# adaLN block with two products: hardware loops written out, the half block's down projection as row pairs

## What is computed

```python
h = layernorm(x) * (1 + ca) + sa
attn = einsum('ds,td->st', w1, w2) * sparse_mask
x = x + ga * gelu(h @ attn + b2)
h = layernorm(x) * (1 + cb) + sb
H = (h @ U1) @ V1 + b1            # U1 1024x256, V1 256x5504
act = silu(H[..., :2752]) * H[..., 2752:]
out = (act @ U2) @ V2 + b2        # U2 2752x256, V2 256x1024
x = x + gb * out
```

## Time and profile before

| what | us |
|---|---|
| median of 3 runs | 1254.88 (1254.66 to 1256.98) |
| the profiled execution | 1254.12 |
| its span, first to last instruction | 1252.3 |
| mean granted TensorE clock over the span | 0.989 of full speed |
| PE busy | 1193.5 (95%), 5617 matmuls |
| DVE busy | 672.5 (54%) |
| ACT busy | 402.4 (32%) |
| POOL busy | 320.1 (26%) |

### The profile page before, as it was taken

One profiled execution on the slowest core, in us unless ns is written; L12 is line 12 of the kernel. 1 busy time (PEld: TensorE's weight loads), 2 busy tenths in 40 slices (PEclk: granted clock), 3 DMA queues, 4 the chain that ended last, 5 costly groups with the idle time before them and its releaser, 6 DMA issues.

```text
span 1252.3 us, 15955 instructions
## 1 busy us (share of the span) xinstructions
PE 1193.5 (95%) x5617; PEld 952.4 (76%) x5617; DVE 672.5 (54%) x1041; ACT 402.4 (32%) x675; POOL 320.1 (26%) x256
## 2 busy tenths in 40 slices
PE   7877999999999899999999999999999999999997
PEld 4445678877786678788888878878877888887885
DVE  0838699999996544543543443353353354345344
ACT  0122334344343364413322313322331332232331
POOL 0023221332323175600420240060060042024014
PEclk9999899999999899999999999999999999999999
DMA  9796635535448464250141042024015013104101
GB/s 344 289 379 243 260 142 195 231 140 223 168 176 301 155 187 170 68 168 1 51 137 49 17 140 80 1 91 144 1 68 169 1 51 135 51 16 140 47 1 68
DMA packets 54064, 165.79 MB, mean 132 GB/s; under 512 B 4976, under 2 KB 9456, under 8 KB 51952
## 3 DMA queue, kind: packets, MB, share of 16 engines
q1 hardware_dynamic: 54000, 164.86, 36.3%
HBM read 122.84 MB, written 42.01 MB: 132 GB/s over the span
## 4 chain that ended last, share of the span: by engine, by line
PE 84%; DVE 8%; DMA 3%; issue 2%; ACT 1%; SPq 1%; POOL 1%; DVEq 0%; ACTq 0%
PE bank L492 26%; PE bank L494 25%; PE bank L493 25%; PE bank L562 4%; DVE nrm L1054 2%; PE bank L658 2%; DMA x<-in_x 2%; PE bank L527 1%; DVE bn L1212 1%; DMA wm_sb<-in_wmod 1%; DVE h_lo L1155 1%; DVE bn L1044 1%; POOL g L1330 1%; DVE xr L1207 1%; ACT h_hi L875 0%
## 5 line engine op out<-in xcount | busy, mean ns | idle before, releaser
L1269 DVE SCALAR_TENSOR_TENSOR act<-bank,b_sb,act 128x512 f32<-128x512 f32 (+1 forms) x176 | 132.0, 750 | 393.3 <-PE bank L494 378.0
L982 ACT ACTIVATE act<-bank,b_sb 128x512 f32<-128x512 f32 (+1 forms) x176 | 121.2, 689 | 516.8 <-PE bank L494 511.8
L492 PE MATMUL bank<-pt,v_hi 128*128 128x512 f32 x688 | 269.4, 392 | 5.9 <-issue 4.4
L493 PE MATMUL bank<-pt,v_hi 128*128 128x512 f32 x688 | 268.4, 390 | 0.0
L494 PE MATMUL bank<-pt,v_lo 128*128 128x512 f32 x688 | 268.4, 390 | 0.0
L1383 POOL TENSOR_TENSOR v_lo<-v2g,v_hi 128x512 fp32r<-128x512 f32 x32 | 41.4, 1294 | 567.8 <-ACT v_hi L998 567.8
L1276 DVE TENSOR_TENSOR act_lo<-act,act_hi 128x512 fp32r<-128x512 f32 (+1 forms) x176 | 172.7, 985 | 0.0
L492 PEld LDWEIGHTS bank<-pt,v_hi 128*128 128x128 f32 x688 | 129.4, 188 | 36.4 <-issue 7.7
L494 PEld LDWEIGHTS bank<-pt,v_lo 128*128 128x128 f32 x688 | 129.5, 188 | 26.9
L493 PEld LDWEIGHTS bank<-pt,v_hi 128*128 128x128 f32 x688 | 129.4, 188 | 26.8
L492 PE MATMUL bank<-act_hi,u_hi 128*128 128x512 f32 (+1 forms) x352 | 139.3, 396 | 1.5 <-DVE act_lo L1276 1.3
(11 more groups left out here) (114 smaller groups left out, 1571.6 us busy)
## 6 DMA issues: line engine op xcount, KB each, us to landing
wm_sb<-in_wmod SPq DMA_DIRECT2D x10, 2048.0 KB, 12.3
xr<-in_x SPq DMA_DIRECT2D x16, 1024.0 KB, 6.8
x_dram<-xr SPq DMA_DIRECT2D x16, 1024.0 KB, 4.3
x2t<-x_dram SPq DMA_DIRECT2D x32, 512.0 KB, 4.0
out<-x2t SPq DMA_DIRECT2D x32, 512.0 KB, 4.7
xs<-in_x SPq DMA_DIRECT2D x7, 2048.0 KB, 8.0
pt_dram<-pt_st SPq DMA_DIRECT2D x8, 1024.0 KB, 3.9
pt<-pt_dram SPq DMA_DIRECT2D x8, 1024.0 KB, 6.8
```

What stands on the lines that cost most here:

```text
L492: nc.tensor.matmul(acc, s_hi, m_hi, start=start, stop=False)
L493: nc.tensor.matmul(acc, s_hi, m_lo, start=False, stop=False)
L982: nc.scalar.activation(act[0:w, i % 2, :], bank[0:w, i % 2, :], ACT.Silu, bias=b1_sb[0:w, i, 0:1]).then_inc(silu_done, 1)
L1269: nc.vector.scalar_tensor_tensor(act[0:w, i % 2, :], up, b1_sb[0:w, i, 1:2], act[0:w, i % 2, :], ALU.add, ALU.mult).then_inc(act_done, 1)
```

## The change

Every `Fori` on every engine becomes a Python `range`: the same instructions are issued, each batch's one behind the other, with constants in place of registers in waits and addresses, and no branch back. In the FFN phase the half block's z product is issued in another form. Today both r use rows 0 to 63 of U2's last block and of act. After the change the second 128 columns of that U2 block lie in rows 64 to 127, and act_hi and act_lo hold the 64 rows twice, in partitions 0 to 63 and 64 to 127. The six matmuls are issued by term, in three pairs: r = 0 on rows 0 to 63 into bank 4, r = 1 on rows 64 to 127 into bank 5. For the copies ACT issues one more act_hi copy and DVE one more act_lo subtraction in each batch, each before the one that raises the semaphore. The last U2 piece is loaded in two parts (64 rows x 128 columns each) instead of one, with one copy (ACT) and one subtraction (POOL) for each.

```diff
--- before.py
+++ after.py
@@ -241,6 +241,7 @@
         raw_in = [sem(f"raw_in{i}") for i in range(3)]
         w_hi_ready = sem("w_hi_ready")
         w_ready = sem("w_ready")
+        half_lo_ready = sem("half_lo_ready")
         pt_in = [sem("pt_in0"), sem("pt_in1")]
         gate_done = sem("gate_done")
         up_done = sem("up_done")
@@ -321,16 +322,21 @@
             parts = [(u2[a:a + full * P, :].rearrange("(i p) r -> p i r", p=P), P, full, R, 0,
                       u2_hi[:, i0:i0 + full, :], u2_lo[:, i0:i0 + full, :])]
             if rest:
-                parts.append((u2[a + full * P:e, :].rearrange("(i p) r -> p i r", i=1), rest, 1, R, full * R,
-                              u2_hi[0:rest, i0 + full:i0 + full + 1, :],
-                              u2_lo[0:rest, i0 + full:i0 + full + 1, :]))
+                for r in range(RB):
+                    cols, rows = slice(r * P, (r + 1) * P), slice(r * rest, (r + 1) * rest)
+                    parts.append((u2[a + full * P:e, cols].rearrange("(i p) r -> p i r", i=1), rows, 1, P, full * R,
+                                  u2_hi[rows, i0 + full:i0 + full + 1, cols],
+                                  u2_lo[rows, i0 + full:i0 + full + 1, cols]))
             pieces.append(parts)
             piece_of["u2", q] = len(pieces)
         PIECES = len(pieces)
+        HALF_PIECE = piece_of["u2", len(GROUPS) - 1] - 1
 
         def raw_part(slot, part):
             _, rows, blocks, n, off, _, _ = part
-            return raw[0:rows, slot, off:off + blocks * n].rearrange("p (k n) -> p k n", k=blocks)
+            if isinstance(rows, int):
+                rows = slice(0, rows)
+            return raw[rows, slot, off:off + blocks * n].rearrange("p (k n) -> p k n", k=blocks)
 
         raw_count = []
         seen = [0, 0, 0]
@@ -418,7 +424,7 @@
                     sp.dma_start(x2_store[b, :, TT // 2:TT, :], xr[:, TT // 2:TT, :]).then_inc(x2_out, 16)
 
             iteration(0, True, False, True, (6, 7, 8, 9))
-            with sp.Fori(1, NB - 2) as b:
+            for b in range(1, NB - 2):
                 iteration(b, True, True, True)
             iteration(NB - 2, True, True, False, (10,))
             iteration(NB - 1, True, True, False, (), True)
@@ -478,7 +484,7 @@
             for n in range(TT):
                 tile_in(0, n)
             batch(0, 0, False)
-            with sp.Fori(1, NB // 2) as i:
+            for i in range(1, NB // 2):
                 batch(i * 2 - 1, 1, False)
                 batch(i * 2, 0, False)
             batch(NB - 1, 1, True)
@@ -737,7 +743,7 @@
 
             iteration(0, True, False, True)
             iteration(1, True, True, True)
-            with pe.Fori(2, NB - 1) as b:
+            for b in range(2, NB - 1):
                 iteration(b, True, True, True)
             iteration(NB - 1, True, True, False)
 
@@ -785,10 +791,18 @@
                     pe.wait_ge(z_lo_ready, b * 2)
                 w = width[i]
                 slot = (q * IB + i) % 4
-                for r in range(RB):
-                    cols = slice(r * P, (r + 1) * P)
-                    last = three(bank[:, 4 + r, :], u2_hi[0:w, i, cols], u2_lo[0:w, i, cols],
-                                 act_hi[0:w, slot, :], act_lo[0:w, slot, :], i == 0, i == IB - 1)
+                if w == P:
+                    for r in range(RB):
+                        cols = slice(r * P, (r + 1) * P)
+                        last = three(bank[:, 4 + r, :], u2_hi[:, i, cols], u2_lo[:, i, cols],
+                                     act_hi[:, slot, :], act_lo[:, slot, :], i == 0, False)
+                else:
+                    terms = ((u2_hi, act_hi), (u2_hi, act_lo), (u2_lo, act_hi))
+                    for t, (weight, moving) in enumerate(terms):
+                        for r in range(RB):
+                            rows = slice(r * w, (r + 1) * w)
+                            last = nc.tensor.matmul(bank[:, 4 + r, :], weight[rows, i, r * P:(r + 1) * P],
+                                                    moving[rows, slot, :], start=False, stop=t == len(terms) - 1)
                 last.then_inc(z_step, 1)
 
             def out_product(b):
@@ -840,7 +854,7 @@
                 pe.wait_ge(lo_ready, turn2(NB - 1) + FB)
                 up_product(0, 0, i)
             batch(0, 0, False)
-            with pe.Fori(1, NB // 2) as i:
+            for i in range(1, NB // 2):
                 batch(i * 2 - 1, 1, False)
                 batch(i * 2, 0, False)
             batch(NB - 1, 1, True)
@@ -968,7 +982,7 @@
             shift_hi(0)
             iteration(0, True, False, True)
             iteration(1, True, True, True)
-            with ae.Fori(2, NB - 1) as b:
+            for b in range(2, NB - 1):
                 iteration(b, True, True, True)
             iteration(NB - 1, True, True, False)
             iteration(NB, False, True, False)
@@ -988,6 +1002,8 @@
                 ae.wait_ge(act_done, b * IB + i + 1)
                 if not at_start(b, i < 4):
                     ae.wait_ge(z_step, b * IB + max(i - 3, 0))
+                if w < P:
+                    nc.scalar.activation(act_hi[w:P, slot, :], act[0:w, i % 2, :], ACT.Copy)
                 nc.scalar.activation(act_hi[0:w, slot, :], act[0:w, i % 2, :], ACT.Copy).then_inc(act_hi_ready, 1)
 
             def v2_hi_part(b, part):
@@ -1016,7 +1032,7 @@
 
             silu(0, 0, 0)
             batch(0, 0, False)
-            with ae.Fori(1, NB // 2) as i:
+            for i in range(1, NB // 2):
                 batch(i * 2 - 1, 1, False)
                 batch(i * 2, 0, False)
             batch(NB - 1, 1, True)
@@ -1245,7 +1261,7 @@
                                     b2_sb[:].unsqueeze(2).to_broadcast([P, FB, NB]), ALU.add).then_inc(table_ready, 1)
             iteration(0, True, False, True)
             iteration(1, True, True, True)
-            with dve.Fori(2, NB - 1) as b:
+            for b in range(2, NB - 1):
                 iteration(b, True, True, True)
             iteration(NB - 1, True, True, False)
             dve.wait_ge(gb_turned, 1)
@@ -1273,6 +1289,9 @@
                 w = width[i]
                 slot = (q * IB + i) % 4
                 dve.wait_ge(act_hi_ready, b * IB + i + 1)
+                if w < P:
+                    nc.vector.tensor_tensor(act_lo[w:P, slot, :], act[0:w, i % 2, :], act_hi[0:w, slot, :],
+                                            ALU.subtract)
                 nc.vector.tensor_tensor(act_lo[0:w, slot, :], act[0:w, i % 2, :], act_hi[0:w, slot, :],
                                         ALU.subtract).then_inc(act_lo_ready, 1)
 
@@ -1302,7 +1321,7 @@
             multiply(0, 0, 1)
             act_lo_part(0, 0, 0)
             batch(0, 0, False)
-            with dve.Fori(1, NB // 2) as i:
+            for i in range(1, NB // 2):
                 batch(i * 2 - 1, 1, False)
                 batch(i * 2, 0, False)
             batch(NB - 1, 1, True)
@@ -1347,8 +1366,15 @@
                 for n, part in enumerate(pieces[m]):
 
                     pool.wait_ge(w_hi_ready, sum(len(p) for p in pieces[:m]) + n + 1)
+                    if not isinstance(part[1], int) and part[1].start:
+                        pool.wait_ge(w_ready, m)
+                        pool.wait_ge(half_lo_ready, n)
                     last = nc.gpsimd.tensor_tensor(part[6], raw_part(m % 3, part), part[5], ALU.subtract)
+                    if m == HALF_PIECE and n < len(pieces[m]) - 1:
+                        last.then_inc(half_lo_ready, 1)
                 last.then_inc(w_ready, 1)
+                if m == HALF_PIECE:
+                    pool.wait_ge(w_ready, m + 1)
 
 
             def iteration(b, has_next):
@@ -1364,7 +1390,7 @@
                 rstd(mv2, ve2, rstd2, mv2_ready, b * 4 + 4, b * 2 + 3 if has_next else b * 2 + 2, rstd2_ready)
 
             iteration(0, True)
-            with pool.Fori(1, NB - 1) as b:
+            for b in range(1, NB - 1):
                 iteration(b, True)
             iteration(NB - 1, False)
 
@@ -1393,7 +1419,7 @@
                     nc.gpsimd.tensor_tensor(half, gbb2_bc[:, h * HALF:(h + 1) * HALF], half,
                                             ALU.add).then_inc(x2_biased, 1)
 
-            with pool.Fori(0, NB) as b:
+            for b in range(NB):
                 gate_v2(b)
                 bias_x2(b)
 
```

## The result

The changed kernel takes **1263.85 us** (median of 4 runs, 1262.04 to 1265.25); the kernel before took 1254.77 beside it (median of 4, 1254.20 to 1256.98). The ratio is 1.0068, 95% interval 1.0054 to 1.0082: slower by 7 to 10 us. The forecast was 1258.8, slower, with 1249 to 1266 as its range. The profiled execution is the slowest of the four: 1265.25 us, span 1263.5, against 1254.12 and 1252.3 before.

What follows compares the result with a forecast made beforehand. TensorE, 84% of the chain, was taken to bound the kernel. Subtractions +13.5, clock +2.3, row pairs -4.7 and loops -6.4 us sum to +4.7 on the profiled 1254.12 us: 1258.8 us, range 1249 to 1266.

Steps and rivals of the forecast that it cites:

- The third subtraction: VectorE's extra act_lo subtraction before the half block, entering TensorE's path in full: 1.69 us a batch, +13.5 us.
- the sum of 15.8 us: Alternative estimate from the skill's port-lock rule for the eight extra VectorE subtractions, 1.97 us each.
- The loops of the FFN phase: TensorE's two FFN loop turns: gaps regained, 4.9 us, and a clock drop avoided, 1.5 us; together -6.4 us.
- Rival (d): Written-out code doesn't help, TensorE waits for instructions elsewhere as often: +11.1 us, 1265.2 us; chance 0.05.
- The pairs: TensorE's half-block products on two 64-row halves at once: 0.59 us gained a batch, -4.7 us in eight.
- The estimate of 0.48: Half-block gain per batch if a row pair gained 1.54x, from the skill's four-tile figure; 3.8 us in eight.
- rival (b): Row halves of the half block's product don't overlap on TensorE: the 4.7 us are missing, 1263.5 us; chance 0.15.
- The ScalarE copy at nothing: ScalarE's extra half-block copy ends while VectorE is busy with block 20: cost nothing; without cover 0.5 us a batch.
- The clock again: TensorE's longer waits before block 21 bring one or two clock drops in eight, 1.5 us each: +2.3, bounds 0 and 12.
- rival (a): The clock holds in every TensorE pause: +2.4 us, 1256.5 us; chance 0.20. Against it, small gaps around each change of shape.
- 4 turns give nothing: TensorE's attention-phase loop turns fall where it waits for normalised rows anyway: no gain; without cover at most 2.4 us.

Runs made afterwards that it cites:

- copies_only: loops_only plus ScalarE's and VectorE's second copy of the half block in every batch, read by nobody, product in its old form: 1281.97 us, ratio 1.0209.
- bias_late: The changed kernel with one more GpSimd wait, so a batch's adds to x2t start only after its last act_lo subtraction: 1244.98 us, ratio 0.9921.
- loops_only: The kernel before with every hardware loop written out as a Python range, nothing else changed: 1249.32 us, ratio 0.9944.
- pe_ffn_loop: The kernel before with only TensorE's FFN loop written out: 1247.84 us, ratio 0.9948.
- order_only: The changed kernel with ScalarE's two half-block copies in the other order, the upper rows' copy with its own semaphore: 1264.35 us, ratio 1.0067.
- bias_late_order: order_only plus the GpSimd wait of bias_late: 1242.13 us, ratio 0.9891.
- filler: The changed kernel with seven useless matmuls on TensorE before its wait for the half block's act_lo: 1258.04 us (median of 7), ratio 1.0028.
- best: bias_late_order with hardware loops back everywhere except TensorE's FFN loop: 1239.98 us, ratio 0.9871.
- pairs_no_copies: The changed kernel without the extra ScalarE copy and VectorE subtraction per batch, output not the wanted one: 1245.33 us, ratio 0.9916.

## Why the prediction was right, and where it was not

**The sign, and its reason, hold.** The time is 5 us above the forecast and inside its range. The third subtraction stands on TensorE's path: forecast 1.69 us a batch, measured 1.67 to 1.68 in the profile after, and copies_only shows the stall without the pairs. That GpSimd's adds make it dear is shown by bias_late, which changes nothing but their time. The rule of the Trainium skill ("SBUF — State Buffer", "SBUF: two separate sides") that the loser waits a whole instruction out would have had 1.97 us, by the estimate of the prediction; the trace has 1.67 between the ends of the two subtractions. That the two engines hold each other up at this place the runs confirm (both are slower together, and both recover in bias_late); the sum of 15.8 us they don't.

**The loops of the FFN phase: right.** -6.4 forecast, -6.5 in loops_only's FFN phase, -6.7 in pe_ffn_loop as a whole. Rival (d) has fallen.

**The pairs: a little undersized.** 0.59 us forecast, 0.71 measured, outside the upper end of 0.68 that I gave: the stream is at that end (three steps of 0.227 instead of six), and the change of shape costs 0.21 instead of 0.24. The two halves of a pair are not 0.11 us apart; they start together. The estimate of 0.48 from the four-tile figure in the section on the span model of "TensorE: Matmul & The Clock Gate" in the Trainium skill is further off: for two 64-row tiles the trace has the stream halved, a gain of 2x. The result lies at rival (b)'s 1263.5, but its mechanism is wrong: pairs do overlap.

**The ScalarE copy at nothing: right**, and for the reason named: VectorE's cover. order_only shows it, and bias_late_order shows its price once that cover is gone: 0.35 us a batch, where 0.5 was written.

**What failed is "The clock again".** It had one or two drops in eight stalls, +2.3 us. The profile has four stalls with drops and +6.2 us against before with the turn's drop counted off, that is 7.7 where 2.3 stood; filler, which takes away all but half of the last one, gains 5.8. I read four pauses of the trace as a rate of one in four and put the new ones near the shorter ones that left the clock alone. They were four single events, two of them longer than the new stall. The count also left out two long pauses: 2.01 us for z_lo in the last batch (start 1237.38), without a drop, and 3.93 us in the attention phase (start 419.75), with one. How little such a count carries is seen at z_lo: all fourteen kernels have this pause of 2.0 us, and eleven of their profiles have a drop near it, best and pairs_no_copies among them, in which no stall for act_lo stands before it. So a part of the last batch's long drop in the changed kernel need not be due to the new stall. That the small gaps named against rival (a) add to the drops isn't shown: filler and pairs_no_copies have the half block's change of shape too, and no drop before the last batch. The bounds, 0 and 12, held the term. Rival (a), no drop at all, is out.

**What was missing: the attention phase.** "4 turns give nothing" was said of time on TensorE and holds for the iterations: they take 38.8 us each in both kernels. That the longer code could cost something elsewhere stands nowhere in the prediction; it has only that turns fall into idle time. It was TensorE's own code, through a DMA store on which VectorE waits: +2.2 us between the two profiles.

With the terms as measured the forecast's sum would read 13.4 + 7.7 - 5.7 - 6.4 + 2.2 = +11.2, the difference of the two profiled executions. The medians differ by 9.1, since the profiled run was the slowest of four: its mean clock is 0.980, that of the fastest run (1262.04) 0.983. On the profiled executions the sum was 6.5 us too low: the clock and the attention phase by 7.6, with 1.1 back from the pairs and the copies. The range took it in because its upper end was set for (b) and (d), neither of which happened; that part is luck.

## What to carry to other kernels

- An instruction added to an engine that is busy 54% of the time can cost its full length, and more than twice its usual one: look at what stands ahead of it on its engine, who waits for it, and what GpSimd does just then. Here the place before the last block was tight already in the kernel before, and one wait that moves GpSimd's adds by 10 us was worth 19 us in the changed kernel and 3.4 us in loops_only, while the row pairs gave 5.6.
- Price a new pause of TensorE with the clock behind it: in this kernel a stall of 1.7 us cost 1.7 and, in three to seven of eight cases, another 1.6 or more. A few pauses of a trace don't give the rate.
- Write out the loop whose turn shows a gap, not all of them.

## What was not expected of the hardware

- Two matmuls of 64 rows in the two halves of the array start together and stream as one: the half block's six products take 0.89 us instead of 1.60, weight loads and the change of shape (0.21 us) included.
- The same 1.7 us stall was followed by clock drops after three, four and six of eight batches in three kernels with pairs behind it, and after seven, some two or three times as long, with six single half-array matmuls behind it (mean clock 0.978 to 0.984 and 0.970 to 0.973). The cause is open.
- A pause of the same length filled with matmuls of no use kept the clock at 1.00 in every batch but the last: 5.8 us for work that computes nothing.
- TensorE's written-out attention loop delayed a 1 MB store from 3.9 to 5.8 us in the profiles of all nine such kernels, and in none of the five where that loop was kept.
